# Projection stage: VectorE computes all four rests of a group, and GpSimd's rotation sums wait for the bias

## The reference, cut to what matters

```python
x = x + scan_layer(layernorm(x))
x = x + moe(layernorm(x))          # 8 experts, the best 2
x = x + attention(layernorm(x))    # W_qkv, rotation of q and k, 16 heads
x = x + moe16(layernorm(x))        # 16 experts, the best 2, and a shared one
# in attention:
Q, K, V = split(einsum('bsi,oi->bso', x, W_qkv))
out = stack([x0 * cos - x1 * sin, x0 * sin + x1 * cos])   # rotation of Q and of K
```

## Time and profile before

| | us |
|---|---|
| median of 3 runs | 1699.57 (1693.02 to 1700.16) |
| profiled execution | 1701.82 |
| its span | 1700.0 |
| TensorE busy | 1514.9 (89%) |
| VectorE busy | 1001.0 (59%) |
| ScalarE busy | 734.0 (43%) |
| GpSimd busy | 595.8 (35%) |

### The profile page before, as it was taken

How to read it: one execution, slowest core, us unless ns; L and a number is a source line. 1 busy time by engine, 2 the same in 40 slices (tenths; PEclk the granted TensorE clock), 3 DMA queues, 4 the chain that set the end, 5 groups by cost and what they waited for, 6 DMA issues and landing times. The chain is left out here.

```text
span 1700.0 us, 31193 instructions
## 1 busy us (share of the span) xinstructions
PE 1514.9 (89%) x9903; PEld 1137.1 (67%) x9903; DVE 1001.0 (59%) x3426; ACT 734.0 (43%) x1537; POOL 595.8 (35%) x1011
## 2 busy tenths in 40 slices
PE   6999999982999999598599999999999587489988
PEld 3777777762899999454276666666666376468876
DVE  3344555443233333389498888888887276545557
ACT  3444444420222222234247777777777232245420
POOL 4123333334222222146733332232333155635520
PEclk9999999985999999799799999999999788689999
DMA  8001111113766667566866666666662475745546
GB/s 226 1 25 41 47 47 48 35 50 101 241 209 217 209 212 212 175 213 210 217 81 95 91 92 92 92 92 92 92 92 49 124 246 191 168 125 159 157 159 192
DMA packets 150592, 221.66 MB, mean 130 GB/s; under 512 B 23648, under 2 KB 98144, under 8 KB 150304
## 3 DMA queue, kind: packets, MB, share of 16 engines
q1 hardware_dynamic: 128672, 170.54, 42.6%
q0 software_dynamic: 13344, 36.52, 6.3%
q10 hardware_dynamic: 8416, 12.60, 2.6%
HBM read 141.12 MB, written 78.21 MB: 129 GB/s over the span
## 5 line engine op out<-in xcount | busy, mean ns | idle before, releaser
L1951 ACT ACTIVATE t_probs<-t_ps_st 128x512 f32<-128x512 f32 x576 | 313.2, 596 | 124.8 <-PE t_ps_st L2003 122.3
L1932 DVE CUSTOM_DVE_ANT_0 whole_sum<-t_ps_s,t_later 128x512 bf16<-128x512 f32 (+3 forms) x512 | 285.7, 587 | 16.4 <-PE t_ps_s L1989 14.3
L1908 POOL TENSOR_SCALAR_AFFINE_SELECT t_probs<-t_probs 128x128 f32<-128x128 f32 x512 | 137.5, 300 | 333.2 <-ACT t_probs L1951 331.5
L1989 PE MATMUL t_ps_s<-t_ks,t_qs 96*128 96x512 f32 (+3 forms) x768 | 247.8, 362 | 0.6 <-ACT t_neg_max L1944 0.5
L2003 PE MATMUL t_ps_st<-t_qs,t_ks 128*128 128x512 f32 (+3 forms) x768 | 242.7, 365 | 0.8 <-ACT t_probs L1951 0.8
L2003 PEld LDWEIGHTS t_ps_st<-t_qs,t_ks 128*128 128x128 f32 x768 | 136.8, 189 | 73.6 <-ACT t_probs L1951 40.2
L1932 DVE CUSTOM_DVE_ANT_0 whole_sum<-t_ps_s,t_later,t_first_max 128x512 bf16<-128x512 f32 (+3 forms) x256 | 140.6, 549 | 48.0 <-PE t_ps_s L1989 48.0
L2018 PE MATMUL t_ps_o<-t_probs,t_vs 128*17 128x256 f32 (+1 forms) x2560 | 154.9, 361 | 0.5 <-ACT whole_sum L1958 0.5
L1989 PEld LDWEIGHTS t_ps_s<-t_ks,t_qs 96*128 96x128 f32 x768 | 138.6, 190 | 18.0 <-DVE t_first_max L1932 1.6
L1337 POOL DMA_INDIRECT outputs_dram<-m_y,m_place x71 | 68.1, 959 | 207.5 <-DVE m_place L1410 199.8
L1367 PE MATMUL m_ps_h<-m_xt,m_w_t 128*128 128x128 f32 x1136 | 140.0, 277 | 0.0
(11 more groups left out here) (324 smaller groups left out, 2708.8 us busy)
## 6 DMA issues: line engine op xcount, KB each, us to landing
m_w_t<-in_w_dram SPq DMA_DIRECT2D x71, 512.0 KB, 3.7
m_x_t<-gathered_dram SPq DMA_DIRECT2D x150, 128.5 KB, 2.7
t_qs<-qkt_dram SPq DMA_DIRECT2D x124, 128.0 KB, 5.4
t_ks<-qkt_dram SPq DMA_DIRECT2D x124, 128.0 KB, 5.6
d_ye<-outputs_dram SPq DMA_DIRECT2D x8, 1024.0 KB, 7.8
qkt_dram<-d_hi ACTq DMA_DIRECT2D x32, 256.0 KB, 3.5
qkt_dram<-d_lo SPq DMA_DIRECT2D x32, 256.0 KB, 5.4
headst_dram<-whole_sum SPq DMA_DIRECT2D x32, 256.0 KB, 7.2
```

The costliest lines, as they stand in the source:

```text
L1908: nc.gpsimd.affine_select(out=diag, in_=diag, compare_op=ALU.is_ge, fill=0.0, base=0, pattern=[[1, P]], channel_multiplier=-1).then_inc(ma ...
L1932: nc.vector.tensor_tensor_reduce(out=seen[:, (NP * p + x) % (RS + 1), 0:keys], in0=bank_of(p, x)[:, 0:keys], in1=masks, scale=1.0, scalar= ...
L1951: nc.scalar.activation(probs[:, p % 2, i // NST, base:base + STC], ps_st[(NX * p + i) % RT][:], ACT.Exp, scale=HD ** -0.5).then_inc(exp_re ...
L1989: nc.tensor.matmul(bank_of(p, x)[:, 0:keys], q[0:MAX_ROW, head, qc * P:(qc + 1) * P], k[0:MAX_ROW, head, k0:k0 + keys], start=True, stop=T ...
```

## The change

VectorE's loop makes all four rests of group t-3 in tick t, ahead of the bias. GpSimd's `rest_late` and its semaphore are removed. In each tick GpSimd, having issued `d_rstd`, waits for `d_bias` before it starts on the four rotation sums. SyncE's stores wait for one semaphore that counts all four rests.

```diff
             def store_lo(g):
                 for n in range(NB):
-                    sp.wait_ge(*((lo_ready, 2 * g + n + 1) if n < 2 else (lo_late_ready, 2 * g + n - 1)))
+                    sp.wait_ge(lo_ready, NB * g + n + 1)
                     sp.dma_start(turned(g, n, 1), lo[:, g % 2, n]).then_inc(qk_stored[g % 2], 16)
...
                 wait(pool, hi_ready, NB * (g - 1) + 2 * which + 2)
-                wait(pool, lo_late_ready if which else lo_ready, 2 * (g - 1) + 2)
+                wait(pool, lo_ready, NB * (g - 1) + 2 * which + 2)
...
-            def rest_late(g):
-                for n in range(2, NB):
-                    pool.wait_ge(hi_ready, NB * g + n + 1)
-                    nc.gpsimd.tensor_tensor(lo[:, g % 2, n, :], qk[:, n, :], hi[:, g % 2, n].bitcast(FP32), ALU.subtract).then_inc(lo_late_ready, 1)
-
...
-            for tick in range(groups + 3):
-                if live(tick - 3):
-                    rest_late(tick - 3)
+            for tick in range(groups + 2):
                 if live(tick):
                     rsqrt(tick)
+                    pool.wait_ge(bias_ready, tick + 1)
                 if live(tick - 2):
...
                 if live(tick - 3):
-                    for n in range(2):
+                    for n in range(NB):
                         rest(tick - 3, n)
```

More of the change, by code:

```diff
@@ L1481, in project_qkv @@
     sum_stored = sem("d_sum_stored")
-    lo_late_ready, ones_filled = sem("d_lo_late_ready"), sem("d_ones_filled")
+    ones_filled = sem("d_ones_filled")
     qk_stored = [sem(f"d_qk_stored{s}") for s in range(2)]
```

## The result

The changed kernel took 1682.36 us in the median of 6 runs (1680.97 to 1686.84), the kernel before 1699.03 (6 runs). The ratio is 0.9913, 95% interval 0.9894 to 0.9932: 0.9% faster, 14.8 us. (The medians lie 16.7 us apart, the means of the same runs, 1683.4 and 1698.1, 14.7.) The profiled execution took 1680.97 us, its span 1679.2. Two later comparisons of the same pair gave 0.9938 (0.9918 to 0.9959) and 0.9951 (0.9931 to 0.9971); the three average 0.9934, 11 us.

The account below looks back on a forecast made before the run. VectorE was taken to bound the projection's loop. Gains of 2.2 us in tick 3 and 7.2 in ticks 4 to 7 made -9.4: 1692.4 against the profiled execution, 1690.2 against the median; range 1683 to 1697.

Parts of the forecast that it names:

- rival "more": Projection stage: first expert sum isn't held and the tail gives its 3 us; 13.6 saved, 1686; chance 0.14.
- Point 1: VectorE's expert sums: with GpSimd's two rests, two held sums per tick go, 2.02 us off; bounds 0 and 2.02.
- Point 2: VectorE's loop: two more rests per tick at 0.64 each, +1.28 us; 1.1 more for each rest meeting GpSimd.
- Point 3: VectorE's wait for GpSimd's rstd before the bias: now covered by the four rests, -0.31 us per tick.
- starved rival: GpSimd's rstd gets in only after the fourth rest; 4.7 us of the gain lost, 1695; chance 0.11.
- Point 4: GpSimd's sums wait for the bias: bias spacing -1.07 us; next tick's first expert sum meets the last rotation sum, +0.30.
- The period: One tick of VectorE's loop: 12.67 us against 14.49, 1.8 off, in ticks 4 to 7.
- The floor: TensorE's time per group where nothing made it wait: 11.83 us, below the new period.
- The tail: Stage's end, DMA engines busy 97%: starts 9.4 us earlier and lasts as long; bounds 0 and 3 us more.
- rival "transfers": Tail's queues start filling at the same moment as before; only 3 us or so gained, 1696 to 1697; chance 0.11.
- rival "slower": GpSimd's late sums run past the rotations, each costing one held instruction, 1.01 us; 5 us slower, 1705; chance 0.05.

Follow-up runs that it names:

- e0: The changed kernel measured a second time beside the kernel before, no edit: 1696.64 against 1705.6 us, ratio 0.9938.
- e7: The changed kernel measured a third time beside the kernel before, no edit: 1695.14 against 1703.47 us, ratio 0.9951.
- e2: The kernel before with only GpSimd's wait for the bias added, two rests staying on GpSimd: ratio 0.9981 to the kernel before.
- e1: The changed kernel without GpSimd's wait for the bias, all four rests on VectorE: ratio 0.9991 to the kernel before.
- e4: The changed kernel with the two rests moved to VectorE computing 4 of their 512 columns: one run, 1692.9 us, before 1703.5.
- e3: The changed kernel with the attention's first eight loads issued by SyncE in tick 5, not ScalarE in tick 8: ratio 0.9914 to the kernel before.
- e6: e3 with the four rotation sums of the last group made by VectorE: 1689.57 us, ratio 0.9928 to the kernel before.
- e5: The kernel before with GpSimd's wait for the bias added and its two rests moved behind it: one run, 1698.4 us, before 1703.5.

## Why the prediction was right, point by point

The forecast was 9.4 us less; the stage gave 11.7, and the three comparisons 14.8, 10.6 and 8.3. Put on the shown median of 1699.57, the ratios make 1684.8, 1689.0 and 1691.2 us against the forecast of 1690.2 and the range of 1683 to 1697; the first comparison's own median, 1682.4, lies 0.6 under that range. The mechanism was right in its main terms. The stage's 11.7 lies halfway between the forecast and the rival "more" (13.6). That the first comparison gave 14.8 was in part luck: the second and third gave less. Only its interval lies wholly beyond the 0.5% of the prediction (0.7 to 1.1% less); those of e0 and e7 reach down to 0.4 and 0.3%.

- **Point 1, the held expert sums.** Right: -2.02 us per tick. e2 keeps GpSimd's rests and keeps both holds, e1 takes the rests away and has rows of 1.66.
- **Point 2, two more rests.** Taken at 1.28; four last 2.41 us in spacing, 0.60 each. The 1.28 of before is the whole row of two rests, 2 x 0.60 and the 0.08 by which a row laps over the next: nothing followed at once there, so the 0.08 stood in the sum, and the prediction doubled it. It is not rstd's doing: two rests with no GpSimd operation beside them have the same row (814.46 in the kernel before, 1.27 us). Right is 2.41 - 1.28 = 1.13.
- **Point 3, rstd.** Right. It waits for the rest that is running and no longer (1.39 for 1.01 us), with four rests as with two. The rests lose nothing to it: four take 2.41 us beside it, 0.60 each. By the Trainium skill's "SBUF — State Buffer", section "Who interferes with whom", the ports that VectorE and GpSimd share are an exclusive lock, and the order of issue decides who blocks. The trace agrees where a large GpSimd operation comes first (the bias, 1.22 for 0.16 us); a small one like rstd, 1.0 us long, held no rest for a time that the rows show. The rows of e1 show what the page left open: at the end of a rest the waiting GpSimd operation goes next, and after it the waiting rest; they alternate, and no side starves. The starved rival is out.
- **Point 4, the bias.** Right: 0.08 us of spacing. The price was 0.30 and measured 0.15: the sums start 0.23 after the bias (793.93, 794.16), and the last sum's row laps over the first expert sums by 0.34 (785.49 + 1.27 against 786.42), but VectorE's row shows only 1.82 - 1.66 = 0.16 of hold. The prediction took the overlap of the rows for the hold.
- **The period.** 12.67 forecast, 12.38 measured: 0.15 from point 2 and 0.15 from point 4.
- **The floor.** Here I was wrong in kind. I wrote that TensorE's floor was below the new period and left it there. But VectorE starts the loop ahead, and TensorE never had to wait for it again: its product for group 7 starts 4.4 us after the end of tick 7's bias (794.08 to 798.47), where before, with TensorE waiting, it was 3.7 (809.74 to 813.44). The bias came 10.9 us earlier relative to the stage's start, the product 10.2. A shorter period still would have given nothing (e4). The period that was better than forecast is thus worth 0.8 us to the product (10.2 for 9.4), not the 1.5 that the bias shows.
- **The tail.** Counted at 0, bounds 0 and 3: 0.8 us from the last full rotations to the attention (33.4 to 32.7), 1.5 from ScalarE's first load. With the DMA share at 0.97 the transfers looked like the bound as said, but not alone: e3 and e6 got 2.1 and 1.0 out of the tail, the latter with the same bytes. The rival "transfers" is out, as the loads moved up with the rest: the first starts 98.2 us after the stage's start, 108.4 before.
- **The rival "slower".** Its price was right: e5 lets two GpSimd operations run past the rotations, and they cost 2.2 us. Its condition was not met: the changed kernel's sums cost the next expert sum 0.15 us.

The 14.8 us of the first comparison are not explained by the stage. They are 3 more than it gave, and the interval of that comparison (11.6 to 18.0) just reaches down to it; the second and third comparison, 10.6 and 8.3, put the excess down to scatter of the other stages.

## What to carry to other kernels

Look for pairs of VectorE and GpSimd operations that both read two tiles from SBUF, and lay GpSimd's beside VectorE operations that read PSUM; one small operation on the critical path, held by a large one, costs as much as the large one's length. Judge the two halves of such an edit together: each alone may only move the hold to the next instruction. And compute the second engine's floor for the whole stage from its first group on, as the period of the first engine says nothing once the second has no gap left.

## What the runs showed of the hardware that was not expected

- The exclusion of VectorE and GpSimd works both ways and alternates: a rotation sum of 1.27 us takes 1.71 beside queued rests, a rest of 0.68 takes 1.75 (e1), and eight rests beside four sums need 9.40 us (e3) where four rests, four sums and four rests on VectorE alone take 7.5 (808.81 to 816.33 in e6).
- The size of the held operation doesn't matter: the bias of 128 x 4 elements took 1.22 us for 0.16, an expert sum of 128 x 256 1.49 for 0.48, a rest of 128 x 512 1.75 for 0.68, each 1.0 to 1.1 more. That of the holding one does: rstd on 128 x 4 elements cost the rests beside it nothing.
- Issuing the eight loads of 128 KB cost ScalarE 7 us, from 1.64 for the first (802.03 in the changed kernel) down to 0.45 for the last, and SyncE in tick 5 of e3 5.4 us, 0.42 to 0.98 each. The DMA share was 1.0 or more in both stretches, so that full queues alone don't explain the long ones; what does was not looked for.
